# The feed-forward part of a gated cross-attention block with its 2048 hidden units on the partitions, without transposes of the hidden tensor, and with both outer convolution taps added by VectorE from PSUM

## The reference

```python
x = x + tanh(g_xattn[0]) * xattn(ctx_2048, layernorm(x), mask, mask, ...)      # 8 heads, T = S = 1024
x = x + tanh(g_ffn[0]) * ffn(layernorm(x), w1, conv_w, conv_b, w2)

def act_quant(x):      # one scale per token
    scale = 127.0 / clip(max(abs(x), axis=-1, keepdims=True), 1e-05)
    return clip(round(x * scale), -128, 127) / scale

def bit_linear(x, w):
    return einsum('bsd,hd->bsh', act_quant(x), weight_quant(w))    # weights become -1, 0, 1 times a scale

def ffn(x, w1, conv_w, conv_b, w2):             # B = 4, S = 1024, D = 512, hidden 2048
    h = bit_linear(x, w1)
    h = depthwise_conv1d(h, conv_w, conv_b)     # per hidden unit, three taps along the tokens, zero padding
    h = silu(h)
    return bit_linear(h, w2)
```

## Time and profile before

| what | value |
|---|---|
| median of 3 runs | 1929.59 us (1925.8 to 1929.66) |
| the profiled execution's own time | 1929.86 us |
| its span, first to last instruction | 1928.0 us |
| busy over the span: PE, DVE, ACT, POOL | 1684.4, 1216.9, 780.3, 729.0 us |
| mean granted TensorE clock | 0.944 |
| part D on DVE: first instruction, end of the span | 1412.75, 1928.0 us |

### The profile page before, as it was taken

How to read it: one execution, slowest core, us unless ns; L and a number is a source line. 1 busy time by engine, 2 the same in 40 slices (tenths; PEclk the granted TensorE clock), 3 DMA queues, 4 the chain that set the end, 5 groups by cost and what they waited for, 6 DMA issues and landing times.

```text
span 1928.0 us, 24398 instructions
## 1 busy us (share of the span) xinstructions
PE 1684.4 (87%) x8738; PEld 1038.8 (54%) x8738; DVE 1216.9 (63%) x2270; ACT 780.3 (40%) x793; POOL 729.0 (38%) x317
## 2 busy tenths in 40 slices
PE   6887899999997699999999999999856785967867
PEld 5666678888885344455445444544433443534434
DVE  6777645343433567755765676465269979799793
ACT  2111122222210044433442344245318766787676
POOL 1121000000000088866885688578606134062340
PEclk9989999999998599999999999999979798997988
DMA  6656547444444511114111412041130030120201
GB/s 233 229 181 206 179 170 243 154 149 152 171 145 152 180 56 56 56 66 143 56 57 66 143 57 100 12 143 35 44 131 1 1 131 0 38 92 0 88 1 44
DMA packets 104676, 200.59 MB, mean 104 GB/s; under 512 B 7568, under 2 KB 27024, under 8 KB 104592
## 3 DMA queue, kind: packets, MB, share of 16 engines
q1 hardware_dynamic: 104592, 199.49, 29.5%
HBM read 127.90 MB, written 71.57 MB: 103 GB/s over the span
## 4 chain that ended last, share of the span: by engine, by line
PE 62%; issue 19%; POOL 7%; DVE 6%; DMA 5%; SPq 1%; ACT 1%; POOLq 0%; DVEq 0%; ACTq 0%
PE ps L1260 13%; PE ps L1272 12%; PE ps L1224 9%; PE ps L1226 9%; PE ps L1225 9%; PE ps L1244 6%; DMA wraw<-in_w2T 5%; POOL h_first L672 4%; POOL h_third L672 2%; PE ps L1285 2%; DVE junk L926 1%; PE ps L1461 1%; DVE h_first L1179 1%; POOL acc L667 1%; DVE gp L1158 1%
## 5 line engine op out<-in xcount | busy, mean ns | idle before, releaser
L667 POOL TENSOR_TENSOR acc<-acc,pr 128x1024 f32<-128x1024 f32 x192 | 457.7, 2384 | 118.7 <-ACT pr L684 99.6
L684 ACT ACTIVATE pr<-ps,mcol 128x1024 f32<-128x1024 f32 x256 | 284.3, 1114 | 405.1 <-PE ps L1260 402.3
L926 DVE CUSTOM_DVE_ANT_0 junk<-ps,mbias 128x512 bf16<-128x512 f32 x512 | 333.4, 689 | 171.8 <-PE ps L1244 168.0
L1272 PE MATMUL ps<-pr,vv 128*64 128x512 f32 x1024 | 273.3, 616 | 0.0
L672 POOL TENSOR_TENSOR h_first<-h_first,last_tap 128x1024 f32<-128x1024 f32 x44 | 104.8, 2385 | 306.2 <-ACT last_tap L804 306.2
L650 POOL MEMSET nmt<- 128x128 f32 x1 | 0.2, 204 | 449.1 <-DMA w_ternary<-wtb 449.1
L1244 PE MATMUL ps<-kh,qh 64*128 64x512 f32 x512 | 136.8, 475 | 26.3 <-DVE nmv L926 17.6
L1244 PEld LDWEIGHTS ps<-kh,qh 64*128 64x128 f32 x512 | 57.5, 193 | 148.3 <-issue 101.7
L1419 PE MATMUL ps<-xiT,w1q 128*128 128x512 bf16 x512 | 125.1, 393 | 5.9 <-ACT xiT L790 5.9
L1461 PE MATMUL ps<-w2q,hq 128*128 128x512 bf16 x512 | 120.8, 390 | 2.5 <-ACT hq L840 1.8
L667 POOL TENSOR_TENSOR acc<-pr 128x1024 f32<-128x1024 f32 x32 | 76.8, 2399 | 110.8 <-ACT pr L684 110.8
(11 more groups left out here) (152 smaller groups left out, 3179.7 us busy)
## 6 DMA issues: line engine op xcount, KB each, us to landing
craw<-in_ctxT SPq DMA_DIRECT2D x8, 2048.0 KB, 9.7
xa<-in_x SPq DMA_DIRECT2D x8, 1024.0 KB, 6.4
wraw<-in_w1T SPq DMA_DIRECT2D x16, 512.0 KB, 7.3
wraw<-in_w2T SPq DMA_DIRECT2D x16, 512.0 KB, 7.6
q_split<-kqh SPq DMA_DIRECT2D x32, 256.0 KB, 2.0
q_split<-kql SPq DMA_DIRECT2D x32, 256.0 KB, 2.3
base<-lna SPq DMA_DIRECT2D x8, 1024.0 KB, 9.1
k_split<-kqh SPq DMA_DIRECT2D x32, 256.0 KB, 2.2
```

Source lines behind the costliest of these rows:

```text
L667: nc.gpsimd.tensor_tensor(acc[:, blk % 2, :], first, pr[:, (8 * blk + j) % NP, :], ALU.add).then_inc(pool_acc, 1)
L684: act.activation(pr[:, u % NP, :], ps[:, 2 * (u % 2):2 * (u % 2) + 2, :].rearrange("p a t -> p (a t)"), ACT.Exp, bias=mcol[:, (u // 64) * ...
L926: dve.tensor_tensor_reduce(out=junk[:, e, :], in0=ps[:, 4 + e, :], in1=mbias[:, b % 2, kk * CH:(kk + 1) * CH], scale=-1.0, scalar=3.0e38, ...
L1272: last = pe.matmul(ps[64 * e:64 * e + 64, 6 + blk % 2, :], vv[:, g % 2, j, 64 * e:64 * e + 64], pr[:, u % NP, e * CH:(e + 1) * CH], start= ...
```

## The change

Part D is written anew; parts A to C keep their instructions. Hidden units now stay on the partitions to the end. The conv loop scales the product in place in PSUM (`scaled`). ACT makes the middle tap from PSUM, and DVE adds both outer taps from PSUM (`first_tap`), so that `gp`, the last tap of ACT and POOL's addition are gone. Silu works in place in SBUF. The tile `hh` holds all 16 results and two slots for maxima. The largest value over the hidden units is taken in two steps: DVE reduces across slots (`highest`), which leaves 128 candidates per token on the partitions; eight transposes turn these (`tops_turned`), and DVE reduces them (`hidden_scales`). TensorE spreads the inverse scales over the partitions (`spread`), DVE multiplies each `hh` slot by them into int8 (`quantised`), and ACT widens int8 to bf16 (`widen`), which TensorE uses directly as weights. The products of a batch are done in the conv loop of the next batch (`product`), those of the last batch at the end (`last_products`). Normalising and scaling up of the layer norm move to POOL and the rounding to ACT, inside the conv loop before it. Residual and output go in tiles of 128 tokens. The hardware loop is unrolled.

```diff
+        TOP = 11
+        SLOT_OF = [j if j < 8 else j + 5 if j < 13 else j - 5 for j in range(KH)]
+        def pair(j):
+            return 2 * (j % 2)
...
+            # POOL: layer norm of the next batch
+            def normal(b, i):
+                nc.gpsimd.tensor_scalar(xn[:, i, :], xn[:, i, :], mv2[:, i, 0:1], rs2[:, 1, i:i + 1], ALU.subtract, ALU.mult).then_inc(pool_nm, 1)
+            def scaled_up(b, i):
+                nc.gpsimd.tensor_scalar(xn[:, i, :], xn[:, i, :], asc[:, i:i + 1], MAGIC, ALU.mult, ALU.add).then_inc(pool_xr, 1)
-                    nc.gpsimd.tensor_tensor(h[j % 3], h[j % 3], last_tap[j % 2][:], ALU.add).then_inc(pool_tap, 1)
...
+            # ACT
+            def taps(b, j):
+                act.wait_ge(dve_g, n + 1)
+                act.activation(hh[:, SLOT_OF[j], :], scaled, ACT.Identity, bias=convb[:, j:j + 1], scale=convw[:, j, 1:2]).then_inc(act_tap, 1)
+            def silu(b, j):
+                act.wait_ge(dve_c0, 2 * (KH * b + j) + 2)
+                act.activation(hh[:, SLOT_OF[j], :], hh[:, SLOT_OF[j], :], ACT.Silu).then_inc(act_silu, 1)
+            def widen(b, j):
+                act.wait_ge(dve_q, KH * b + j + 1)
+                act.activation(hq[:, j, :], q8[:, j % 4, :], ACT.Copy).then_inc(act_hq, 1)
...
+            # DVE
+            def scaled(b, j):
+                dve.wait_ge(pe_h, n + 1)
+                dve.tensor_tensor(banks, banks, row[:], ALU.mult).then_inc(dve_g, 1)
+            def first_tap(b, j):
+                dve.wait_ge(act_tap, n + 1)
+                dve.scalar_tensor_tensor(out=hh[:, SLOT_OF[j], 1:S], in0=banks[:, 0:S - 1], scalar=convw[:, j, 0:1], in1=hh[:, SLOT_OF[j], 1:S],
+                                         op0=ALU.mult, op1=ALU.add).then_inc(dve_c0, 1)
+                dve.wait_ge(dve_c0, 2 * n + 1)
+                dve.scalar_tensor_tensor(out=hh[:, SLOT_OF[j], 0:S - 1], in0=banks[:, 1:S], scalar=convw[:, j, 2:3], in1=hh[:, SLOT_OF[j], 0:S - 1],
+                                         op0=ALU.mult, op1=ALU.add).then_inc(dve_c0, 1)
+            def highest(b, slots, cols, out, ready, before):
+                dve.tensor_reduce(out, hh[:, slots, cols].rearrange("p j t -> p t j"), AX.X, ALU.max, apply_absolute_value=True).then_inc(dve_mx, 1)
+            # highest_first: 4 x (8 slots, 256 tokens); highest_rest: 2 x (6 slots, 512) and 2 x (4 slots, 512)
+            def quantised(b, j):
+                if n >= 4:
+                    dve.wait_ge(act_hq, n - 3)
+                dve.tensor_tensor(q8[:, j % 4, :], hh[:, SLOT_OF[j], :], ps[:, 6:8, :].rearrange("p a t -> p (a t)"), ALU.mult).then_inc(dve_q, 1)
...
+            # PE
+            def spread(cols, bank):
+                for i in range(NT):
+                    last = pe.matmul(ps[:, bank + i // 4, i % 4 * P:(i % 4 + 1) * P], cols[:, i:i + 1].broadcast_to([P, P]), ident[:],
+                                     start=True, stop=True)
+            def hidden(b, j):
+                if j >= 2:
+                    pe.wait_ge(dve_c0, 2 * (n - 1))
...
+            for b in range(B):
+                for j in range(KH):
+                    if b:
+                        product(NT * (b - 1) + j // 2, j % 2)
+                    if j + 2 < KH:
+                        hidden(b, j + 2)
+                if b + 1 < B:
+                    for u in range(NT // 2):
+                        turn_xi(b + 1, u)
+                tops_turned(b)
+                pe.wait_ge(dve_hm, 5 * b + 4)
+                spread(hsc, 6).then_inc(pe_inv, 1)
+                if b + 1 < B:
+                    scale_row(b + 1)
+                    hidden(b + 1, 0)
+                    hidden(b + 1, 1)
+            last_products()
```

More of the change, by code:

```diff
@@ L21 @@
 BF16 = mybir.dt.bfloat16
+INT8 = mybir.dt.int8
 ALU = mybir.AluOpType
@@ L216, in flamingo_gated_block @@
         hdq = sb("hdq", [P, NT], F32)
-        row = sb("row", [P, S], F32)
+        assert used["at"] <= 229344
         assert used["at"] <= 229344
@@ new lines, in silu @@
+            def silu(b, j):
[3 more added lines that the diff above has]
+                act.wait_ge(dve_q, KH * b + j + 1)
+                if b and j == 0:
+                    act.wait_ge(pe_o, NT * b)
+                act.activation(hq[:, j, :], q8[:, j % 4, :], ACT.Copy).then_inc(act_hq, 1)
+            deviation(0)
+            for i in range(NT):
+                integers(0, i)
@@ new lines, in _ @@
+            for u in range(NT // 2):
+                turned(0, u)
+            scale_row(0)
+            for b in range(B):
+                for j in range(KH):
+                    taps(b, j)
+                    if j >= 2:
+                        silu(b, j - 2)
+                    if b + 1 < B:
+                        if j == 4:
+                            deviation(b + 1)
+                        for i in INTS.get(j, ()):
+                            integers(b + 1, i)
+                silu(b, KH - 2)
+                silu(b, KH - 1)
+                if b + 1 < B:
+                    for u in range(NT // 2):
+                        turned(b + 1, u)
+                    scale_row(b + 1)
+                for j in range(KH):
+                    widen(b, j)
@@ L1210, in _, with statistics @@
-            for step in ln_steps(dve, 0):
-                step()
-            for s in range(3):
-                dve.memset(gp[:, s, 0:1], 0.0)
-                dve.memset(gp[:, s, S + 1:S + 2], 0.0)
-            with dve.Fori(0, B - 1) as b:
-                ffn(b, True)
-            ffn(B - 1, False)
+            def statistics(b, i):
+                if i == 0:
+                    dve.wait_ge(sp_xn, 16 * (b + 1))
+                dve.bn_stats(st2[:, i, :], xn[:, i, :]).then_inc(dve_st, 1)
@@ L1220, in split_mm @@
+            for k in range(NT * (B - 1), NT * B):
+                finish(k)
         def split_mm(pe, acc, lhs, rhs, n):
@@ L1227, in split_mm @@
             return last
-        def ln_row(pe, b):
-            pe.wait_ge(dve_ln, b * LN_DVE_N + LN_DVE["diag"])
-            for t in range(2):
-                last = pe.matmul(ps[:, 2 + t, :], ones[:], diag[:, 4 * t:4 * t + 4, :], start=True, stop=True)
-            last.then_inc(pe_row, 1)
         def c_pe(pe):
@@ new lines, in scale_row @@
+            def scale_row(b):
+                pe.wait_ge(dve_sc, 4 * b + 4)
+                spread(adq, 2).then_inc(pe_row, 1)
+            def hidden(b, j):
+                n = KH * b + j
+                if j >= 2:
+                    pe.wait_ge(dve_c0, 2 * (n - 1))
+                elif j == 0 and b:
+                    pe.wait_ge(dve_hm, 5 * b - 4)
+                elif j == 1:
+                    pe.wait_ge(act_row, b + 1)
+                if j == 0:
+                    pe.wait_ge(act_xt, 4 * b + 4)
+                for t in range(2):
+                    for k in range(KD):
+                        last = pe.matmul(ps[:, pair(j) + t, :], w1q[:, k, j * P:(j + 1) * P], xiT[:, k, t * CH:(t + 1) * CH],
+                                         start=k == 0, stop=k == KD - 1)
+                last.then_inc(pe_h, 1)
@@ new lines, in product, with tops_turned @@
+            def product(k, part):
+                i = k % NT
+                if part == 0:
+                    pe.wait_ge(act_hq, KH * (k // NT + 1))
+                    if i >= 2:
+                        pe.wait_ge(dve_o, k - 1)
+                for j in range(8 * part, 8 * part + 8):
+                    last = pe.matmul(ps[:, OUT_BANK[k], :], hq[:, j, i * P:(i + 1) * P], w2q[:, j, :], start=j == 0, stop=j == KH - 1)
+                if part:
+                    last.then_inc(pe_o, 1)
+            def tops_turned(b):
+                pe.wait_ge(dve_mx, 8 * (b + 1))
+                pe.wait_ge(dve_c0, 2 * KH * (b + 1))
+                for i in range(NT):
+                    last = pe.transpose(ps[:, i // 4, i % 4 * P:(i % 4 + 1) * P], tap[:, 0, i * P:(i + 1) * P], ident[:])
+                last.then_inc(pe_top, 1)
```

514 lines of the change are left out of this document (209 added, 305 removed).

## The result

| | kernel before | changed kernel |
|---|---|---|
| median | 1928.51 us (1925.8 to 1929.66, 4 runs) | 2062.53 us (2056.36 to 2064.48, 4 runs) |
| ratio, 95% interval | | 1.069, 1.067 to 1.072 |
| span of the profiled execution | 1928.0 us | 2062.7 us |

What follows compares the result with a forecast made beforehand. DVE was taken to bound the conv loop, PE to be busiest in the second stage. Start 1445.6, batch 0 156.5, batches 1 and 2 149.1 each, batch 3 165.3 reach 2065.6; with 1.86 around the span, 2067 us, range 1985 to 2100.

Steps and rivals of the forecast that it cites:

- Conv group: Conv loop: DVE's own work per group, one scaling and two taps from PSUM, sums to 3.73 us, against 4.05 before.
- Round trip: Conv loop: DVE idles about 2.06 us per group while PE refills the banks its taps freed; a group costs 5.79 us.
- Rival D: Conv loop: DVE's wait for PE's product is covered in some unseen way, giving near 2007 us; chance 0.05.
- Maxima at 1.88 ns an element: DVE's stepped reductions across slots, in and behind the loop: 3.99 us for 2048 elements, 5.92 for 3072.
- rival A: Maxima across slots: the step costs nothing, rate 1.04 ns an element, giving 2004 us; chance 0.26.
- Clock: Batch 0's conv loop: PE's low clock costs 1.7 us in each of ten groups without a maximum, 17, taken as 12.
- rival B: Conv loops of batches 1 to 3: TensorE's clock stays low there too, giving 2112 us; chance 0.08.
- Start: Part D's beginning: first scaling at 1444.5 instead of 1441.49, bounds 1440 and 1450, with POOL's 16 scalings in the chain.
- Gap: Between two conv loops: maxima, turn, reductions, spread, quantisations and next scaling, uncovered on DVE, sum to 49.7 us; before, 47.9.
- End: Last batch: remaining products, x2 loads, last addition and store finish 37.5 us after quantisation began.
- Rival C: DVE's new passes take two elements per cycle, making the kernel faster than before, 1867 us; chance 0.02.

## Why the prediction was right, point by point

The mechanism held, and so did the size of its main terms; that the sum of 2065.6 came within 3 us of the span of 2062.7 is luck, for errors of both signs cancel in it. The sum starts a batch behind its first scaling; cut in the same way, the terms are:

| stretch | forecast, us | measured, us | difference |
|---|---|---|---|
| to behind the first scaling | 1445.6 | 1454.2 | +8.6 |
| conv loops, batches 0 to 3 | 106.8, 99.4, 99.4, 99.4 | 109.8, 97.8, 100.3, 99.6 | +2.5 |
| gaps, batches 0 to 2 | 49.7 each | 44.7, 45.0, 44.7 | -14.7 |
| gap of batch 3, up to its quantising | 28.4 | 25.1 | -3.3 |
| end | 37.5 | 41.4 | +3.9 |

- **Conv group, 3.73 us.** Held: 3.63 without a wait, with three pairs. Scaling in place in PSUM takes 1.23 us, no more than into SBUF.
- **Round trip, 2.06 us.** Held and shown: 5.73 us a group at full clock against 5.79, and the third pair of banks, which touches nothing else, gives 70 us of part D back. Rival D is out.
- **Maxima at 1.88 ns an element.** Right in kind, 10% high: (3.644 - 0.14) / 2048 = 1.71 ns, 3.64 and 5.36 us against 3.99 and 5.92. That the step is the cause is shown by the kernel that reads neighbours, at 1.04; rival A is out. (Its price had a slip: behind a loop 2 x 2.58 + 2 x 1.72 are 8.6 us, not 8.9, so A stood at 2005, not 2004.) Of the two pages of the Trainium skill weighed there, the runs agree with the 16-byte penalty of "SBUF — State Buffer", section "Door 1: The DMA port swizzle". The result per cycle of "VectorE: DVE Perf Modes", section "Mode 1× (REGULAR) — the baseline", doesn't hold for this step: 1.71 ns an element against 1.04.
- **Clock, +12 us in batch 0.** The term mis-sized on the low side. The ten groups without a maximum took 73.9 us (1454.76 to 1528.69), 7.39 each; forecast were 57.9 + 12. So the low clock cost 16 us and not 12. The four groups with a maximum took 29.2 us against 30.5: eight matmuls at the low clock (3.6 us) fit beside a maximum of 3.64, so there it cost nothing. My step from 17 down to 12, for groups that might be at full clock, had no row behind it; the idle of 3.83 us is close to the 4.29 after which the clock had been low. In later batches it was mixed (0.86 in batch 1), and the loops came out at the forecast; rival B (low throughout) is out.
- **Start, 1444.5.** Too early by 8.6 us, and outside its bounds (1440 to 1450). 2.3 are the part's later start. The rest is POOL: I bounded each of its scalings by 0.64 and 1.19 us, but the one with two operands per partition takes 2.07; eight of them are 16.5 us. The other kind, 0.695, was inside.
- **Gap, 49.7 us.** 44.7: the maxima 17.7 instead of 19.8, the spread 3.74 instead of 4.6, and ScalarE late by 0.2 at most instead of 2.1; the quantising took 18.19 against 18.1. Five us less, three times, and 3.3 in the last batch: this paid for the start and the clock.
- **End, 37.5 us.** 2062.7 - 2021.32 = 41.4. The loads of x2 end five waits of 1.5 to 2.4 us each; I had placed them but counted them once. With eight buffers 5 to 7 us were won.
- **Rival C**, two elements a cycle, is out: no DVE pass with PSUM or two tensors was under 1.04 ns.

What stays open: why the part's start moves by up to 7 us between profiles with the same work ahead of it, and how much of batch 0's low clock depends on the gap's length, for which no two kernels differ in that alone.
